# Causal mask of the self-attention scores: added by VectorE instead of by a product on TensorE

## What is computed

```python
q = q * cos + _rotate_half(q) * sin
k = k * cos + _rotate_half(k) * sin
att = jnp.einsum('bhqd,bhkd->bhqk', q, k) / math.sqrt(hd)
mask = jnp.triu(jnp.full((T, T), -jnp.inf, dtype=att.dtype), k=1)
att = jax.nn.softmax(att + mask, axis=-1)
out = jnp.einsum('bhqk,bhkd->bhqd', att, v)
...
x = _layernorm(x + _L0_attn_ref(x, L0_attn_Wq, L0_attn_Wk, L0_attn_Wv, L0_attn_Wo), axis=-1)
x = _layernorm(x + _L0_xattn_ref(x, ctx_2048, mask_BxS2_bk0), axis=-1)
x = _layernorm(x + _L0_ffn_ref(...), axis=-1)
```

## Time and profile before

| what | value |
|---|---|
| median of 3 runs | 1427.34 us (1425.03 to 1430.05) |
| profiled execution, its own time | 1426.88 us |
| its span, first to last instruction | 1425.2 us |
| TensorE busy | 1296.4 us, 91% |
| VectorE busy | 833.9 us, 59% |
| ScalarE busy | 713.1 us, 50% |
| GpSimd busy | 380.9 us, 27% |
| mean granted clock of TensorE | 0.963 of full |

### The profile page before, as it was taken

One profiled execution on the slowest core, in us unless ns is written; L12 is line 12 of the kernel. 1 busy time (PEld: TensorE's weight loads), 2 busy tenths in 40 slices (PEclk: granted clock), 3 DMA queues, 4 the chain that ended last, 5 costly groups with the idle time before them and its releaser, 6 DMA issues. The chain is left out here.

```text
span 1425.2 us, 22213 instructions
## 1 busy us (share of the span) xinstructions
PE 1296.4 (91%) x7473; PEld 1031.0 (72%) x7473; DVE 833.9 (59%) x1773; ACT 713.1 (50%) x1592; POOL 380.9 (27%) x484
## 2 busy tenths in 40 slices
PE   5899999999999889999999997989999999899970
PEld 4666776766776478888888886777888878688850
DVE  6777677677766676666767666782333323233327
ACT  4788578667857744453545444213333333233324
POOL 0234124224312220100101001002553554455430
PEclk9999999999999899999999999999999999999995
DMA  5311212211200127687777576147989889886648
GB/s 192 119 53 46 74 54 81 75 46 45 74 24 31 70 88 238 223 276 247 254 248 270 179 244 242 41 152 270 270 197 318 256 219 311 254 211 107 111 69 338
DMA packets 91067, 235.59 MB, mean 165 GB/s; under 512 B 10632, under 2 KB 47500, under 8 KB 86224
## 3 DMA queue, kind: packets, MB, share of 16 engines
q1 hardware_dynamic: 73120, 188.96, 37.3%
q0 software_dynamic: 17840, 45.22, 15.6%
HBM read 146.20 MB, written 87.95 MB: 164 GB/s over the span
## 5 line engine op out<-in xcount | busy, mean ns | idle before, releaser
L2056 PE MATMUL e_both_ps<-e_w,e_x_t 128*128 x948 | 241.1, 402 | 0.0
L2056 PEld LDWEIGHTS e_both_ps<-e_w,e_x_t 128*128 128x128 f32 x948 | 172.6, 189 | 36.3
L539 PE MATMUL proj_ps<-wqkv,x_sp 128*128 128x384 f32 x768 | 172.9, 354 | 10.7 <-DVE wqkv L424 10.6
L1922 POOL DMA_INDIRECT acc_rows<-e_y,token_row x79 | 125.6, 1590 | 171.4 <-ACT e_y L1966 76.6
L1228 PE MATMUL c_score_ps<-ct,x_t 128*128 128x402 f32 x768 | 158.4, 359 | 0.0
L1253 PE MATMUL c_out_ps<-cr,weigh_t 128*128 128x512 f32 (+1 forms) x624 | 146.6, 393 | 1.4 <-DVE weigh_t L1050 1.4
L316 POOL TENSOR_SCALAR_AFFINE_SELECT p_t<-p_t 128x128 f32<-128x128 f32 x256 | 87.8, 356 | 218.8 <-ACT p_t L402 215.0
L1228 PEld LDWEIGHTS c_score_ps<-ct,x_t 128*128 128x128 f32 x768 | 140.5, 193 | 5.5 <-issue 4.2
L1991 DVE TENSOR_TENSOR e_x_t<-e_turn_ps,e_x_t 128x512 fp32r<-128x512 f32 x79 | 54.5, 691 | 152.5 <-ACT e_x_t L1953 152.5
L539 PEld LDWEIGHTS proj_ps<-wqkv,x_sp 128*128 128x128 f32 x768 | 130.9, 193 | 12.7 <-issue 11.2
L2079 PE MATMUL e_down_ps<-e_w,e_h_t 128*128 x474 | 126.4, 402 | 9.4 <-DVE e_h_t L2003 9.4
(11 more groups left out here) (232 smaller groups left out, 2251.3 us busy)
## 6 DMA issues: line engine op xcount, KB each, us to landing
e_w<-w_split SPq DMA_DIRECT2D x15, 3072.0 KB, 12.3
w_split<-c_piece SPq DMA_DIRECT2D x96, 384.0 KB, 4.0
c_piece<-w_experts SPq DMA_DIRECT2D x96, 192.0 KB, 3.9
raw<-ctxT SPq DMA_DIRECT2D x16, 800.5 KB, 4.3
w_split<-rows SPq DMA_DIRECT2D x24, 512.0 KB, 3.5
raw<-ctx_rows SPq DMA_DIRECT2D x16, 768.0 KB, 5.7
acc_rows<-rows SPq DMA_DIRECT2D x8, 1024.0 KB, 8.5
rows<-w_experts SPq DMA_DIRECT2D x24, 256.0 KB, 2.7
```

What stands on the lines that cost most here:

```text
L539: mm = nc.tensor.matmul(proj_ps[:, tt, 0:GW], x_sp[:, xs, c, tt * P:(tt + 1) * P], wqkv[:, ws, c, hg * GW:(hg + 1) * GW], start=(c == 0 an ...
L1922: nc.gpsimd.indirect_dma_start(acc[m % 2], bass.IndirectOffsetOnAxis(ap=token_row[:, 1, m:m + 1], axis=0), y[:, m % YB, :], None, compute_ ...
L2056: mm = nc.tensor.matmul(both_ps[:, m % 2, :], x_t[:, m % 2, xs, c * P:(c + 1) * P], weights(slot, ws, c * GU, (c + 1) * GU), start=(c == 0 ...
```

## The change

The product with the mask goes; the score product then ends its own accumulation. In its place VectorE adds `mask_qk` to the diagonal block in PSUM, in place, and waits for that addition (semaphore `masked`) before it reduces the row. The bf16 identity, which only the mask product read, goes with the two GpSimd instructions that made it. To make room for the new semaphore, each of the three layer norms gives up one: setting EPS now counts on `aggregated`.

```diff
-        ident_b = sb("ident_b", [P, P], BF16)
...
-            nc.gpsimd.memset(ident_b[:, :], 1.0).then_inc(const_pool, 1)
             nc.gpsimd.memset(mask_qk[:, :], 0.0).then_inc(const_pool, 1)
-            pool.wait_ge(const_pool, 3)
-            for m in (ident, ident_b):
-                nc.gpsimd.affine_select(out=m[:, :], in_=m[:, :], compare_op=ALU.is_equal, fill=0.0,
-                                        base=0, pattern=[[-1, P]], channel_multiplier=1).then_inc(const_pool, 1)
-
+            pool.wait_ge(const_pool, 2)
+            nc.gpsimd.affine_select(out=ident[:, :], in_=ident[:, :], compare_op=ALU.is_equal, fill=0.0,
+                                    base=0, pattern=[[-1, P]], channel_multiplier=1).then_inc(const_pool, 1)
...
-            dve.wait_ge(const_pool, 6)
+            dve.wait_ge(const_pool, 4)
...
                         if n == 0:
                             dve.wait_ge(max_lo, g)
                             dve.wait_ge(row_exped, g * NS)
+                        diagonal = row_place(n)[:, qt * P:(qt + 1) * P]
+                        nc.vector.tensor_tensor(diagonal, diagonal, mask_qk[:, :], ALU.add).then_inc(masked, 1)
+                        dve.wait_ge(masked, g * NS + n + 1)
                         nc.vector.tensor_reduce(neg_row_max[:, qt, h:h + 1], row_place(n)[:, 0:(qt + 1) * P],
                                                 AX, ALU.max, negate=True).then_inc(maxed, 1)
...
                     nc.tensor.matmul(place[:, 0:wide], q_st[0:3 * HD, h, qt * P:w],
-                                     k_st[0:3 * HD, h, 0:wide], start=True, stop=False)
-                    nc.tensor.matmul(place[:, w - P:w], ident_b[:, :], mask_qk[:, :],
-                                     start=False, stop=True).then_inc(scored, 1)
+                                     k_st[0:3 * HD, h, 0:wide], start=True, stop=True).then_inc(scored, 1)
...
         if b == 0:
-            nc.vector.memset(eps[:, :], EPS).then_inc(eps_set, 1)
+            nc.vector.memset(eps[:, :], EPS).then_inc(aggregated, 1)
...
-        act.wait_ge(eps_set, 1)
-        act.wait_ge(aggregated, parts[b][1])
+        act.wait_ge(aggregated, 1 + parts[b][1])
```

More of the change, by code:

```diff
@@ L120, in self_attention @@
         turned, q_stacked, k_stacked = sem("turned"), sem("q_stacked"), sem("k_stacked")
-        scored, maxed, max_hi, max_lo = sem("scored"), sem("maxed"), sem("max_hi"), sem("max_lo")
+        scored, masked, maxed, max_hi, max_lo = sem("scored"), sem("masked"), sem("maxed"), sem("max_hi"), sem("max_lo")
         max_turned = sem("max_turned")
@@ L681, in layer_norm @@
     half_v = ctx.enter_context(nc.sbuf_tensor(name + "_half_v", [P, NT], F32))
-    eps_set, gathered, aggregated = sem(name + "_eps_set"), sem(name + "_gathered"), sem(name + "_aggregated")
+    gathered, aggregated = sem(name + "_gathered"), sem(name + "_aggregated")
     rooted, inverted, normed = sem(name + "_rooted"), sem(name + "_inverted"), sem(name + "_normed")
@@ L705, in normalise @@
         mine = slice(*parts[b])
-        dve.wait_ge(aggregated, parts[b][1])
+        dve.wait_ge(aggregated, 1 + parts[b][1])
         nc.vector.tensor_scalar(half_v[:, mine], mean_var[:, mine, 1], EPS, -0.5, ALU.add, ALU.mult
```

## The result

The changed kernel takes 1455.55 us (median of 3 runs, 1453.2 to 1460.17) against 1427.34: a ratio of 1.0196, 95% interval 1.017 to 1.0222. The forecast was 1461 us in a range of 1442 to 1479. The profiled execution is the longest of the three, 1460.17 us with a span of 1458.4.

The account below looks back on a forecast made before the run. Self-attention was taken as balanced, TensorE full and VectorE's chain ending about as late. With additions VectorE ends last: the groups' lengthenings sum to 34.2 us, 1426.9 + 34.2 = 1461 us, range 1442 to 1479.

Parts of the forecast that it names:

- The bound: Self-attention's row scores: TensorE full, VectorE's chain ending about as late; its 2.3 us idle a group will not suffice.
- The removed products: TensorE, self-attention: 256 mask products of 0.064 us go, 1.0 us a group, counting only where TensorE ends last.
- The price of an addition: VectorE, before each row reduction: 0.34 us with its wait, bounded by 0.22 from below and 0.40 from above.
- The eight ordinary groups: Self-attention groups like 9: VectorE's chain takes 13.93 us against 11.32, each group 2.5 us longer.
- Groups 4, 8 and 12: Self-attention groups followed by 48 output products covering VectorE's tail: only step 15's score counts, 1.9 us longer each.
- Group 0: First self-attention group, without weight pieces or the scaling of a group before (L212): 0.9 us longer.
- The groups 1, 13, 14 and the last: Self-attention groups with fewer weight pieces or no projections between scores: 2.1, 1.9, 1.5 and 2.1 us longer.
- Nothing takes it back: Behind self-attention: cross-attention's loads move along, so everything later keeps its length, some 34 us later.
- The first: Self-attention: additions fall into VectorE's idle time, only the removed masks count, 1411 us; chance 0.03.
- The second: Self-attention: TensorE's waits spread half-clock spells, 13 to 26 us on top, 1474 to 1487 us; chance 0.12.
- The third: Wait inside VectorE is free, an addition costs 0.22 us: 6.1 us longer in all, 1433 us; chance 0.08.
- The fourth: VectorE writing PSUM is dearer, 0.40 us an addition: 15 us more, 1476 us; chance 0.17.

Follow-up runs that it names:

- e6: Changed kernel with each VectorE mask addition done twice, the second waiting for the first: 1544.24 us, ratio to before 1.0816.
- e1: Changed kernel without its additions and without mask products, so row scores carry no mask: 1415.14 us, ratio to before 0.991.
- e2: Changed kernel with the mask product put back on TensorE, so both engines mask: 1466.79 us, ratio to before 1.0255.
- e8: Changed kernel with sums written to an SBUF tile nobody reads and the reduction not waiting for the addition: 1434.14 us, ratio to before 1.0053.
- e9: Changed kernel with sums written to an SBUF tile nobody reads, the reduction still waiting for the addition: 1456.82 us, ratio to before 1.0213.
- e4: Changed kernel with VectorE adding only in steps 2, 4, 6 and 12, TensorE multiplying in the other twelve: 1438.5 us, ratio to before 1.0075.
- e7: Changed kernel with addition and row maximum in one VectorE instruction, exp scale -1: 1420.38 us, ratio to before 0.9949.

## Why the prediction was right, step by step

- **The bound.** Right: the stage was balanced, and the chain of row maxima took over. 2.3 us of idle time a group for 16 additions did not suffice. e6 shows that every 0.33 us more then counts in full. TensorE's waits for exps begin earlier than forecast, not in the third block of scores but in the first two: 0.70 us at step 7.
- **The removed products.** Right in direction, too small in size: 0.064 us a product forecast, 0.09 measured as TensorE's busy time (e1 against before, e2 against after), 1.5 us a group and not 1.0. They count where TensorE ends last (e1, 11 us), little where VectorE does (e2, 0.28 us a group), so the error hardly reached the forecast. The sum counted the earlier start, 0.08, which the timeline has (0.42 us behind the first score and not 0.50 as before).
- **The price of an addition.** This is the term that was a little large: 0.34 us forecast, 0.32 to 0.34 measured and mostly 0.32 to 0.33, since the additions last 0.29 and not 0.30. Over 16 steps this is the difference between the chain of 13.93 us that was forecast and the 13.68 measured, and 13.68 - 11.32 - 0.08 = 2.28 is the 2.26 us that an ordinary group grew. Neither bound came true: 0.22 was close to e8's case (0.19 to 0.21), 0.40 nobody's.
- **The eight ordinary groups** were forecast at 20.0 us and gave 17.3. Besides the price above (1.9 of the 2.7 us), group 5 was 0.8 longer than its neighbours already before, with a granted clock of 0.94. This part of the miss is chance: the trace that was forecast from had a spell there, the one after had none.
- **Groups 4, 8 and 12** gave 1.52 instead of 1.9. Thirteen of the smaller additions explain 0.2 of that; the other 0.2 was not followed up.
- **Group 0** was the one clear miss: 1.84 us instead of 0.9. The sum took the two weight pieces and L212 off a chain without idle time. But the chain there is broken: between the exps of steps 7 and 8 ScalarE prepares a piece of weights for 1.90 us (L345, the former L349), and TensorE waits 1.72 us before step 11's score for the exp behind it. The trace of before had this wait already, 1.25 us long, and the sum overlooked it. So the new price is paid on either side: from the first score to step 11's the group is 0.86 us longer, from there to the transposes 0.77. The remaining 0.2 lies ahead of the first score, where the granted clock over the first 5 us of the group was 0.50 after and 0.71 before; it is not part of the change. ScalarE's piece of weights and TensorE's step 11 after, then TensorE's before:

```profile
39.80 1.90 ACT L345 ACTIVATE wo<-rows 128x2048 fp32r<-128x2048 f32 x1
```

```profile
42.32 0.44 PE L560 MATMUL den_ps<-k_st,q_st 96*128 96x384 f32 x1 [1.72 <-ACT den_ps L374]
```

```profile
39.64 0.44 PE L561 MATMUL den_ps<-k_st,q_st 96*128 96x384 f32 x1 [1.25 <-ACT den_ps L378]
```

- **The groups 1, 13, 14 and the last** were within 0.31 us of the forecast, all below it.
- **Nothing takes it back.** Right: the router's first product (L1757, the former L1761) starts 34.75 us later in the profiled pair, the whole span is 33.2 longer. Between the last transposes and that product lie 385.1 us after and 382.6 before; the ten traces, of kernels alike in that stretch, scatter from 382.3 to 385.4.
- **The rivals.** The first (TensorE stays the bound) falls with e6. The second (the clock) did not come with this change: 0.98 over the stage, as before; it did with twice the additions. The third is e8's kernel, 22.7 us below the same kernel with the wait (e9). The fourth falls with e9.

In all 34.2 us were forecast and 30.6 measured in the stage: the mechanism was right. The difference is the addition's price and the spell in group 5 (together 2.7 in the ordinary groups), 1.1 in groups 4, 8 and 12 and 0.7 in groups 1, 13, 14 and the last, less the 0.9 that group 0 added.

## What to carry to other kernels

Where two engines share a pipeline through a few buffers, the busier one is not the one to unload until the other's chain has been laid out end to end: here products that fill TensorE for 1.5 us a group were taken away, and 5.2 us came to a chain with 2.3 us of idle time. Count an operation between producer and consumer at its full latency, its own wait included, even where the engine that does it is idle beforehand (e4). If VectorE must do it, put it into the pass that is made anyway (e7).

## What the runs showed of the hardware

- A VectorE instruction that waits for the one directly ahead starts 0.32 us after it, for 128 columns, and without the wait 0.20, while the durations in the profile stay the same (e8, e9). Over 256 instructions the wait was worth 22.7 us.
- An addition of 128x128 from PSUM lasts as long into PSUM in f32 (0.29, changed kernel) as into SBUF in bf16 (0.28 to 0.29, e8 and e9).
- A product of 128 columns that adds the mask fills TensorE for 0.09 us, between score products and projections (e1 and e2, 16 of them in a group).
- One VectorE instruction that adds a mask, writes PSUM and reduces costs 0.02 to 0.05 us more than the reduction alone at 512 columns (e7: 0.62 to 0.65 against 0.60), and shows as two rows, the second the read of the accumulator (0.14).
